# Attention and a two-expert feed-forward block on one core: the query projection moves to the key side, and a slot takes two heads

## What is computed

```python
Q = xn @ Wq + bq ; K = xn @ Wk ; V = xn @ Wv      # 16 heads of 64
R = xn @ Wr + br                                    # 16 heads of 10
d = t - p ; valid = (d >= 0) & (d < 128)            # a window of 128 positions
extra[h,t,p] = sum_n R[h,t,n] * b_nd[n, d]          # 0 where not valid
logits = Q @ K.T / 8 + where(valid, 0, -1e9) + extra
out = softmax(logits) @ V  -> (heads side by side) @ Wproj + bproj
# experts: router logits xn @ router_w.T, the two best of 8, softmax over the two,
# each gelu(xn @ w1.T + b1) @ w2.T + b2, summed with those weights
```

## Time and profile before

| engine | busy us | share of the span | instructions |
|---|---|---|---|
| PE matmul | 1577.5 | 94% | 11947 |
| PE weight load | 1363.3 | 81% | 11947 |
| DVE | 1155.8 | 69% | 4444 |
| ACT | 1092.7 | 65% | 3774 |
| POOL | 760.6 | 45% | 1418 |

### The profile page before, as it was taken

One profiled execution on the slowest core, in us unless ns is written; L12 is line 12 of the kernel. 1 busy time (PEld: TensorE's weight loads), 2 busy tenths in 40 slices (PEclk: granted clock), 3 DMA queues, 4 the chain that ended last, 5 costly groups with the idle time before them and its releaser, 6 DMA issues.

```text
span 1677.3 us, 49343 instructions
## 1 busy us (share of the span) xinstructions
PE 1577.5 (94%) x11947; PEld 1363.3 (81%) x11947; DVE 1155.8 (69%) x4444; ACT 1092.7 (65%) x3774; POOL 760.6 (45%) x1418
## 2 busy tenths in 40 slices
PE   3755999999999999999999998999999999999998
PEld 3424888888888888888999997888888888888886
DVE  4486888887787788872221112888888888888887
ACT  2223777777777777774555443777777777777775
POOL 1231566665565656660000000655555556555555
PEclk7696999999999999999999998999999999999999
DMA  9775555656555555545666665555555555555552
GB/s 284 255 269 151 167 153 164 172 171 174 159 164 173 171 151 152 165 138 184 198 204 198 210 208 159 158 165 168 163 159 156 152 158 162 161 170 162 169 151 76
DMA packets 384742, 290.34 MB, mean 173 GB/s; under 512 B 17666, under 2 KB 359092, under 8 KB 384692
## 3 DMA queue, kind: packets, MB, share of 16 engines
q1 hardware_dynamic: 376500, 272.95, 54.8%
q0 software_dynamic: 8192, 16.79, 3.4%
HBM read 167.96 MB, written 113.26 MB: 168 GB/s over the span
## 4 chain that ended last, share of the span: by engine, by line
PE 72%; issue 19%; DVE 4%; SPq 2%; DMA 1%; ACT 1%; DVEq 0%; POOL 0%; ACTq 0%; POOLq 0%
PE ps L1275 13%; PE ps L1408 12%; PE ps L1277 10%; PE ps L1276 10%; PE ps L1389 10%; PE ps L1378 7%; PE ps L1420 6%; PE ps L1347 4%; DVE gst L1028 1%; SPq L390 1%; SPq L444 1%; DMA wproj<-in_L_attn_Wproj_dram 1%; DMA xn_d<-xn 0%; DVE xn L905 0%; PE ps L1202 0%
## 5 line engine op out<-in xcount | busy, mean ns | idle before, releaser
L793 ACT ACTIVATE prob<-logit,low 128x128 f32<-128x128 f32 (+1 forms) x1024 | 459.0, 449 | 301.4 <-DVE low L1073 300.6
L658 POOL TENSOR_SCALAR prob<-prob,inv 128x128 f32<-128x128 f32 x512 | 192.3, 376 | 752.8 <-DVE inv L1063 731.9
L1073 DVE CUSTOM_DVE_ANT_0 logit<-ps,extra 128x128 f32<-128x128 f32 (+1 forms) x1024 | 321.0, 351 | 133.6 <-PE ps L1277 113.0
L1085 DVE COPY probT<-ps 128x384 f32<-128x384 f32 x512 | 283.0, 553 | 3.0 <-PE ps L1389 2.8
L1389 PE MATMUL ps<-ident,prob 128*128 128x128 f32 x1536 | 251.5, 272 | 2.5 <-DVE probT L1085 1.0
L660 POOL TENSOR_SCALAR prob<-prob,inv 128x256 f32<-128x256 f32 x512 | 244.7, 478 | 0.0
L1408 PE MATMUL ps<-probT,val 128*64 128x256 f32 (+1 forms) x2048 | 223.0, 339 | 0.0
L1028 DVE TENSOR_TENSOR gst<-ps,gbias 128x512 f32<-128x512 f32 x256 | 175.8, 687 | 39.4 <-PE ps L1347 20.8
L1378 PEld LDWEIGHTS ps<-xnT,qry 128*128 128x128 f32 x1024 | 184.2, 190 | 21.9 <-issue 0.3
L766 ACT ACTIVATE qry<-ps,qbias 128x128 f32<-128x128 f32 x512 | 182.1, 356 | 23.1 <-PE ps L1277 23.0
L1378 PE MATMUL ps<-xnT,qry 128*128 (+1 forms) x1024 | 196.9, 273 | 0.0
(11 more groups left out here) (185 smaller groups left out, 3439.4 us busy)
## 6 DMA issues: line engine op xcount, KB each, us to landing
skew<-gst SPq DMA_DIRECT2D x256, 256.0 KB
extra<-skew SPq DMA_DIRECT2D x128, 512.0 KB, 3.9
extra<-skew SPq DMA_DIRECT2D x128, 256.0 KB, 2.9
w1b<-w_d SPq DMA_DIRECT2D x39, 514.0 KB, 3.6
w2b<-w_d SPq DMA_DIRECT2D x39, 320.0 KB, 3.4
x_place<-zero SPq DMA_DIRECT2D x39, 256.0 KB, 2.8
placed<-x_place SPq DMA_DIRECT2D x39, 256.0 KB, 3.9
y_place<-yrow SPq DMA_DIRECT2D x39, 256.0 KB, 2.3
```

The source lines that it names most:

```text
L658: nc.gpsimd.tensor_scalar(prob[:, h % 4, 0:P], prob[:, h % 4, 0:P], inv[:, h % 4, 0:1], 1.0, ALU.mult, ALU.mult).then_inc(norm_made, 1)
L793: nc.scalar.activation(prob[:, h % 4, a:b], logit[:, h % 2, a:b], ACT.Exp, scale=-1.0, bias=low[:, h % 2, t:t + 1], accum_out=total[:, h % ...
L1073: ins = nc.vector.tensor_tensor_reduce(out=logit[:, h % 2, a:b], in0=ps[:, S_BANK[h % 2], a:b], in1=extra[:, h % H, a:b], scale=1.0, scala ...
L1085: nc.vector.tensor_copy(probT[:, h % 4, :], ps[:, PT_BANK, 0:3 * P]).then_inc(pT_made, 1)
```

## The change

- **Keys instead of queries.** wm is transposed, and one `keys` per pair of heads makes wm x xq for both heads in one bank (6 matmuls of 256 columns). ACT copies all 512 columns once as the high part, DVE subtracts once for the low part. The logits have xq as the stationary operand, and one product serves two heads: tile 0 is three float32r matmuls of 2 x 128 columns into S0_BANK, tile 1 three of 2 x 256 columns into S1_BANK. The plain float32 matmul is gone.
- **Biases.** qbias and gbias, their matmuls and their ACT copies go. xq is now xn + 1 (POOL, one more instruction per sequence), and Wq, Wk, Wv and Wr are centred over their input rows so that the constant 1 carries the biases: DVE reduces and corrects wqT and wkT, three matmuls with a matrix of ones give the sums of Wv and Wr, and wm waits for the first, the splits of Wv and Wr for the second.
- **Slots.** `sequence` has 8 slots, one per pair; each has keys for j+1, the transposes of the odd head of j-3, the logits of j, value product of j-3, output product of j-4, and at its end the transposes of the even head of j-2. LAG is 4 slots of a pair. `prob` has 8 buffers instead of 4, `logit` 4 instead of 2.
- **Units.** The table is new, with two places per slot. The g of tile 1 are copied out by ACT, those of tile 0 by DVE, both without an addition; the rounding of r goes from DVE to POOL. The first value unit of a sequence is made one sequence ahead.
- **Moved or gone.** `copy_x` and xg are gone (values read xq). ADDS becomes (1, 2). POOL's indirect DMAs go to slots (2, 3, 3, 4, 5, 6, 6, 7). Loops take two sequences per turn.

The diff, cut to what the text speaks of:

```diff
-        UNITS = [(0, "v", 0, 0, 0), (1, "v", 0, 1, 0), (2, "g", 2, 1, 0), (3, "g", 3, 0, 0), (4, "g", 3, 1, 0),
-                 (5, "v", 1, 0, 0), (6, "v", 1, 1, 0), (7, "r", 0, 0, 1), (8, "r", 1, 0, 1), (10, "g", 0, 0, 1),
-                 (11, "g", 0, 1, 1), (12, "g", 1, 0, 1), (13, "g", 1, 1, 1), (15, "g", 2, 0, 1)]
-        LAG = 7
-        ADDS = (2, 4)
+        KEY_BANK, S1_BANK, S0_BANK, PT_BANK, HEAD_BANK, MISC_BANK, OUT_BANK = 0, (1, 2), 3, 4, 5, 6, 7
+        UNITS = [(0, 0, "g", 2, 1, 0), (1, 0, "r", 0, 0, 1), (1, 1, "g", 3, 0, 0), (2, 0, "v", 0, 1, 0),
+                 (3, 0, "g", 3, 1, 0), (3, 1, "v", 1, 0, 0), (4, 0, "g", 0, 0, 1), (4, 1, "g", 0, 1, 1),
+                 (5, 0, "v", 1, 1, 0), (5, 1, "r", 1, 0, 1), (6, 0, "g", 1, 0, 1), (6, 1, "g", 1, 1, 1),
+                 (7, 0, "v", 0, 0, 1), (7, 1, "g", 2, 0, 1)]
+        UNITS_FINAL = [unit for unit in UNITS if not unit[5]]
+        START = [("r", 0, 0), ("r", 1, 0), ("g", 0, 0), ("g", 0, 1), ("g", 1, 0), ("g", 1, 1), ("v", 0, 0), ("g", 2, 0)]
+        LAG = 4
+        MOVES = (2, 3, 3, 4, 5, 6, 6, 7)
+        ADDS = (1, 2)
...
+            def keys(i, par, pair):
+                wait_from(pe, key_low, i * PAIRS + pair)
+                for n in range(2):
+                    h = 2 * pair + n
+                    mm = product(ps[:, KEY_BANK, n * T:n * T + T],
+                                 ((wm_hi[:, h, :], wm_lo[:, h, :]), (xq_hi[:, par, :], xq_lo[:, par, :])))
+                mm.then_inc(key_psum, 1)
+            def turn_probs(i, h):
+                pe.wait_ge(norm_made, 2 * (i * H + h + 1))
+                wait_from(pe, pT_made, i * H + h)
+                for n in range(3):
+                    mm = nc.tensor.transpose(ps[:, PT_BANK, n * P:(n + 1) * P],
+                                             prob[:, h % PB, n * P:(n + 1) * P], ident[:, :])
+                mm.then_inc(pT_psum, 1)
+            def logits(i, par, pair):
+                pe.wait_ge(key_low, i * PAIRS + pair + 1)
+                wait_from(pe, logit0_made, i * PAIRS + pair)
+                product(ps[:, S0_BANK, 0:T].rearrange("p (n k) -> p n k", n=2),
+                        ((xq_hi[:, par, 0:P], xq_lo[:, par, 0:P]),
+                         (key_hi[:, pair % 2, :, 0:P], key_lo[:, pair % 2, :, 0:P]))).then_inc(s0_psum, 1)
+                wait_from(pe, logit_made, i * PAIRS + pair - 1)
+                product(ps[:, S1_BANK[pair % 2], :].rearrange("p (n k) -> p n k", n=2),
+                        ((xq_hi[:, par, P:T], xq_lo[:, par, P:T]),
+                         (key_hi[:, pair % 2, :, :], key_lo[:, pair % 2, :, :]))).then_inc(s1_psum, 1)
+            def sequence(i, par, start, heads=True, more=True):
+                for j in range(PAIRS if heads else LAG):
+                    if heads and (j + 1 < PAIRS or more):
+                        keys(i if j + 1 < PAIRS else i + 1, par if j + 1 < PAIRS else 1 - par, (j + 1) % PAIRS)
+                    if here(i, j - 3, heads, start):
+                        turn_probs(i, 2 * (j - 3) + 1)
+                    if heads:
+                        logits(i, par, j)
+                        units(i, par, j, 0, more)
...
+                        pe.wait_ge(pT_made, i * H + 2 * pair + 2)
...
+                    if here(i, j - 4, heads, start):
+
+                        pair = j - 4
+                        pe.wait_ge(head_made, i * PAIRS + (pair + 1))
...
+                    if here(i, j - 2, heads, start):
+                        turn_probs(i, 2 * (j - 2))
+                    if heads:
+                        units(i, par, j, 1, more)
...
+            def keys(i, pair):
...
+                nc.scalar.copy(key_hi[:, pair % 2, :, :].rearrange("p n k -> p (n k)"),
+                               ps[:, KEY_BANK, :]).then_inc(key_high, 1)
...
+                for j in range(PAIRS if heads else LAG):
+                    if heads and (j + 1 < PAIRS or more):
+                        keys(i if j + 1 < PAIRS else i + 1, (j + 1) % PAIRS)
+                    for n, kind, k, t, ahead in units_at(j, 0, more) if heads else []:
+                        unit(len(START) + i * len(UNITS) + n, kind, k, t, i + ahead)
+                    if heads:
                         for t, (a, b) in enumerate(((0, P), (P, 3 * P))):
+                            act.wait_ge(logit0_made if t == 0 else logit_made, i * PAIRS + (j + 1))
+                            for h in (2 * j, 2 * j + 1):
...
+                        ins.then_inc(prob_made, 1)
+                    if here(i, j - 3, heads, start):
...
+            for w, sums, g in ((wqT, qsum, "wq"), (wkT, ksum, "wk")):
+                dve.wait_ge(prep_high, FIRST[g] + 2)
+                nc.vector.tensor_reduce(sums[:, :], w[:, :, :], AX_X, ALU.add).then_inc(wq_centred, 1)
...
+                for j in range(PAIRS if heads else LAG):
+                    pair = j - 1
+                    if here(i, pair, heads, start):
+
+                        h = 2 * pair % PB
+                        dve.wait_ge(prob_made, i * PAIRS + pair + 1)
+                        wait_from(dve, norm_made, 2 * (i * H + 2 * pair + 2 - PB))
+                        nc.vector.reciprocal(inv[:, h:h + 2, :], total[:, h:h + 2, :]).then_inc(inv_made, 1)
+                    if here(i, j - 3, heads, start):
+                        copy_probs(i, 2 * (j - 3) + 1)
+                    if heads and (j + 1 < PAIRS or more):
+                        keys(i if j + 1 < PAIRS else i + 1, (j + 1) % PAIRS)
+                    if heads:
...
                         for t, (a, b) in enumerate(((0, P), (P, 3 * P))):
+                            wait_apart(dve, s0_psum if t == 0 else s1_psum, i * PAIRS + j + 1, const_made)
...
+                            for h in (2 * j, 2 * j + 1):
...
+                            ins.then_inc(logit0_made if t == 0 else logit_made, 1)
+                    for n, kind, k, t, ahead in units_at(j, 0, more) if heads else []:
+                        if kind == "g" and t == 0:
+                            positions(len(START) + i * len(UNITS) + n, i + ahead, k, t)
+                    if here(i, j - 2, heads, start):
...
+                        copy_probs(i, 2 * (j - 2))
...
```

More of the change, by code:

```diff
@@ new lines, in build, with units_at, unit_taken @@
+        MOVES = (2, 3, 3, 4, 5, 6, 6, 7)
+        MOVES_FINAL = (1, 1, 2, 2, 3, 3, 4, 4)
+        ADDS = (1, 2)
+        def units_at(slot, place, more):
+            table = UNITS if more else UNITS_FINAL
+            return [(n, kind, k, t, ahead) for n, (at_slot, at_place, kind, k, t, ahead) in enumerate(table)
+                    if at_slot == slot and at_place == place]
+        def unit_taken(engine, kind, k, t, seq):
+            if kind == "v":
+                engine.wait_ge(val_made, 4 * seq + (2 * k + t + 1))
+            elif kind == "r":
+                engine.wait_ge(r_copied, 2 * seq + (k + 1))
+            elif t == 1:
+                engine.wait_ge(g_act, 4 * seq + (k + 1))
+            else:
+                engine.wait_ge(g_dve, 4 * seq + (k + 1))
@@ L727, in _ @@
             prep_copy(FIRST["brev"], brev[:, :], bank(FIRST["brev"], NB, WIN), -1.0)
-            for k in range(GROUPS):
-                prep_copy(FIRST["gb"] + k, gbias[:, k * BANK:(k + 1) * BANK], bank(FIRST["gb"] + k))
-            for k in range(2):
-                prep_copy(FIRST["qbias"] + k, qbias[:, k, :], bank(FIRST["qbias"] + k, P, PAIRS), -SCALE)
             for k in range(4):
@@ L800, in sequence @@
                         act.wait_ge(head_psum, i * PAIRS + (pair + 1))
-                        wait_from(act, out_psum, i * PAIRS + (pair - 1))
+                        wait_from(act, out_psum, i * PAIRS + pair - 1)
                         nc.scalar.copy(headT[:, pair % 2, :], ps[:, HEAD_BANK, 0:T]).then_inc(head_made, 1)
+                    for n, kind, k, t, ahead in units_at(j, 1, more) if heads else []:
+                        unit(len(START) + i * len(UNITS) + n, kind, k, t, i + ahead)
@@ L823, in _ @@
                 s1 = s0 + HALF
-                for k in range(2):
-                    weights(s0 * len(UNITS) + k, s0 * 2 + k, k)
-                queries(s0, 0)
+                for n, (kind, k, t) in enumerate(START):
+                    unit(s0 * len(UNITS) + n, kind, k, t, s0)
+                keys(s0, 0)
                 sequence(s0, s0)
-                with act.Fori(s0 + 1, s1 - 1) as i:
-                    sequence(i, s0)
+                with act.Fori(0, HALF // 2 - 1) as m:
+                    sequence(2 * m + (s0 + 1), s0)
+                    sequence(2 * m + (s0 + 2), s0)
                 sequence(s1 - 1, s0, more=False)
@@ L1088, in sequence @@
+                    for n, kind, k, t, ahead in units_at(j, 1, more) if heads else []:
+                        if kind == "g" and t == 0:
+                            positions(len(START) + i * len(UNITS) + n, i + ahead, k, t)
```

(18 more changed lines are left out.)

442 lines of the change are left out of this document (195 added, 247 removed).

## The result

The changed kernel takes 1712.1 us (median of four runs, 1710.5 to 1715.9) against 1681.1 for the one before in the same series: ratio 1.0189, 95% interval 1.0170 to 1.0207. I had 1680, range 1654 to 1704: it is 31 us slower than the kernel before where I expected no difference, and 8 above the top of my range. The profiled execution is the slowest of the four, 1715.9.

What follows compares the result with a forecast made beforehand. PE's own instructions were taken as the bound; its 28 us saving would be given back by waits. 1679.1 - 6 - 3.5 - 3 + 12 + 1 = 1679.6, taken as 1680 us, range 1654 to 1704.

Steps and rivals of the forecast that it cites:

- What PE saves per pair: Logits of a pair of heads on PE fall from 1.16 to 1.05 us: 0.88 a sequence, 28 over 32.
- Rival 3: PE's saving is below 0.11 a pair, say 0, from gaps in the float32r product: 1707 at most; 0.25 shared with the ring.
- (a): PE waits for the transposes' one PSUM bank after slots 0 and 2: 0.2 us each, 0.4 a sequence.
- (b): PE waits for the units' one bank in slots 4 and 6: 0.05 us each, 0.1 a sequence, bounds 0 and 0.5.
- (c): Second stage: DVE's row additions delay copies for value products in slots 2 and 3: 0.5 and 0.8, 1.3 us a sequence.
- Head and tail: Stage ends and starts: seven waits of 0.9 us per tail; +12 for two tails, bounds 0 and +16, +1 for heads.
- Preparation: Before the first stage: bias matmuls go, but SP's stores limit the gain; together -3 us, bounds -8 and +2.
- The sum: All terms added to the profiled execution of 1679.1 us: 1679.6, taken as 1680; own case has chance 0.5.
- the rivals, 1: The new slot's waits don't appear and PE stays full: 1655 us, chance 0.25.
- the ring through ScalarE and VectorE: Softmax chain from key copy to exponentials decides slots 0, 4 and 6: 1700 us; 0.25 shared with Rival 3.

Runs made afterwards that it cites:

- run 1: The changed kernel with VectorE and ScalarE looping one sequence per turn again, TensorE and GpSimd still two: 1681.2 us, ratio to the kernel before 1.0009.
- run 11: run 1 plus end-of-stage banks, swapped units of slots 4 and 6, units of slots 0 and 2 in place 1, earlier second-stage additions: 1638.7 us (0.9751).
- run 8: run 1 with the units of slots 0 and 2 moved from place 0 to place 1: 1664.9 us (0.9918).
- run 7: run 1 with the two position units of slots 4 and 6 swapped, ScalarE's copy in place 0: 1672.5 us (0.9956).
- Run 6: run 1 with the last sequence's transposes of heads 9, 11, 13 and 14 in free PSUM banks, ahead of the value product: 1667.8 us (0.9936).
- run 10: run 1 with VectorE's second-stage additions of fetched rows ahead of the even head's copy in slots 1 and 2: 1671.4 us (0.9941).
- run 3: The kernel before with VectorE and ScalarE looping two sequences per turn, nothing else changed: 1709.5 us (1.0187).
- run 5: The changed kernel, loops still doubled, with 122 filler waits added at the start of ScalarE's program and 180 on VectorE's: 1704.4 us (1.0145).
- run 12: run 5 with 66 filler waits at the start of VectorE's program in place of 180, ScalarE's 122 kept: 1734.5 us (1.0325).

## Why the prediction was wrong

**The step that failed** is the one that is missing. I named every instruction that the diff adds to or takes from a slot, and passed over the three lines that make each loop take two sequences. I treated them as costing nothing: no sentence gives them a price, and none of my rivals is about them. They cost 31 us (run 1), which is nearly the whole error. "If the sequences come out under 37.2 or over 38.5 I am wrong" did catch it, in the sequences behind a branch.

Two things were there to be seen. The page before has the q14 line, and the kernel before has VectorE bodies of 252 and 275 instructions and no such stall in its trace, so that a doubled body was a state that no row covered and wanted a bound from both sides, as I gave other unseen costs. And the Trainium skill, Runtime: NRT & Kernel Launch, section "Instruction fetch mechanics", says that an engine's instruction memory holds 512 instructions (2048 on TensorE), is filled in blocks of 256 ahead of the program counter, and that a branch to a block no longer there stops the engine until it is fetched. By that TensorE's 1237 were safe and VectorE's 406 a risk. The runs agree with the direction and with TensorE. They also go further than the page. A body of 406 does not exceed 512. If two blocks of 256 were at hand, then wherever VectorE's program begins, at least one of the four places tried would have the body of 406 inside two blocks; it stalled at all four. So that code is fetched again at the branch is shown by the idle time, by its going with the doubling, and by the packets (93 to 136 with VectorE's long bodies, 58 with ScalarE's alone, 25 and 26 with neither); the rule by which it happens stays open.

**What PE saves per pair**: the total is right, its parts are not, and that they cancel is luck. Run 11 has sequences of 37.20 with no wait in them; 38.04 - 0.88 is 37.16. Counted from start to start over one sequence of the first stage, run 11 against the kernel before, keys and logits take 15.1 us against 16.6, so 1.5 less where I had 0.88; transposes take 4.0 against 6.0. But outputs cost 4.4 against 2.9 and units of kind g 2.6 against 1.9. I had these three unchanged, and I have not tested what sets them. Rival 3, that the logits would save less than 0.11 a pair, is out.

**(a) One bank for the transposes**: 0.4 forecast, 0.48 in the timeline of run 1; by run 8 0.3 to 0.6, by what it is compared with. Right.

**(b) The one bank for units**: mis-sized. 0.1 forecast, 0.5 measured in the timeline (0.38 in slot 4, 0.13 in slot 6) and by run 7 in the first stage. It is my upper bound. This is most of why the first stage takes 38.15 and not 37.66. It varies: in the traces of runs 6 and 10 it is 0.27, 0.14 in slot 4 and 0.13 in slot 6, and that is why they have 38.0; what makes it longer in run 1 is not known.

**(c) `add_rows`**: mis-sized the other way. 1.3 forecast; second-stage sequences are 0.35 longer than first-stage ones, and run 10 takes 0.5 off. One wait before a value product appears, not two. With (b), this gives a second stage of 38.50 where I had 38.96. I had also taken 39.18, one sequence, for the second stage before, where most take 39.27.

**Head and tail**: seven waits per tail were right, 0.65 to 0.74 each and not 0.9, so 4.9 and not 6.5 per stage. Run 6 takes off 10 at the two ends, with a wait of 0.41 left in each. What the ends cost in all is in the table below.

**Preparation**: SP's first store of xn starts at 58.77 in run 1 against 60.54, as forecast (58.3), but the first position copy of the first stage comes at 164.83 against 163.74. One trace decides little here: in the nine traces of the changed kernel's preparation and unchanged first slots that copy comes at 162.6 to 165.4, in the two of the old preparation (before and run 3) at 163.7 and 164.6. Of -3 nothing is seen, and where it goes I have not found.

**The sum.** My terms, 1680, meet run 1 (1681.2) by luck. Read by ScalarE's exponentials (L793 before, L826 in run 1), the profiled execution of run 1 against the one before has:

| stretch | before, us | run 1, us | difference | my term |
|---|---|---|---|---|
| up to the first exponential | 155.2 | 157.0 | +1.8 | -3 |
| first stage | 602.0 | 600.0 | -2.0 | -6 |
| last of the first stage to first of the second | 291.2 | 299.5 | +8.3 | |
| second stage | 617.4 | 604.7 | -12.7 | -3.5 |
| last exponential to the end | 11.6 | 17.5 | +5.9 | |

The third and the fifth together are +14.3, where I had +13 for head and tail. So the errors are +5, +4, +1 and -9, and +1 is left.

Of the rivals, 1 had the right length of a sequence without waits, and 2, the ring through ScalarE and VectorE, never decided: in run 11 the slots are on average 0.12 shorter still ((38.15 - 37.20) / 8) and TensorE does not wait.

## What to carry to other kernels

When a diff changes how much code one turn of a loop holds, count the compiled instructions per engine, waits included, and price the branch; look at the instruction queue's line of the page. Double the body only on the engine whose code needs it; VectorE's and ScalarE's did not. When one wait is gone from a bank or ring, look for the next one at the same place by the time from start to start, since waits of 0.1 to 0.4 us hardly show in the list of waits, and edits at them gave 9 and 16 us here.

## What was not expected of the hardware

- Instructions that do nothing moved the time by 30 us: 1704 to 1735, by where they put VectorE's loop body. Part of it is the clock: in the loops' long sequences it fell four times in the trace of run 5 (1704), and in that of run 12 (1735) at all six branches of the first stage, five times for 6.8 us. Each instruction packet is 8.2 KB (1.04 MB in 127), and between 200 and 700 us, with six branches back, the kernel with ScalarE's stall gone (run 5) loads 35 of them.
- A stall of 2.2 us can cost TensorE 1.4 more, through some 3 us at a granted clock of 0.50 that begin after it has resumed. It did behind seven of twelve such stalls.
- ScalarE's stall of 2 us cost only 0.5 us at each of its six branches (3.3 in all), VectorE's 2.3 at each of twelve (27.6, slow clock included). TensorE's wait at the branch is for VectorE's copy of the transposes (the 2.18 above); that ScalarE's exponentials are wanted later is how I read it, not tested.
